# Layer four's attention: one VectorE operation a head for mask term and maximum, half the shift on GpSimd, scores one unit ahead

## What is computed

```
def attention(q, k, v, mask):                      # NH = 16 heads of HD = 16
    scores = einsum('bhqd,bhkd->bhqk', q, k) / sqrt(HD)
    scores = scores * mask - 10000.0 * (1.0 - mask)
    probs = softmax(scores, axis=-1)
    return einsum('bhqk,bhkd->bhqd', probs, v)
x = hidden + attention(self)  @ w_ao + b_ao
x = x      + attention(cross) @ w_co + b_co
return x + gelu(layernorm(x) @ w1 + b1) @ w2 + b2
```

## Time and profile before

| | us |
|---|---|
| median of 3 runs | 2088.03 (2087.43 to 2091.12) |
| the profiled execution | 2083.72 |
| its span, first to last instruction | 2082.0 |
| TensorE busy in the span | 1866.2 (90%) |
| VectorE busy | 1156.5 (56%) |
| ScalarE busy | 971.2 (47%) |
| GpSimd busy | 778.5 (37%) |

### The profile page before, as it was taken

The page is one execution under the profiler, slowest core; times in us unless marked ns, Lnnn a source line. Parts: engine busy times, 40 slices in busy tenths (PEclk is TensorE's granted clock), DMA queues, the critical chain, the costliest instruction groups (busy, mean ns, idle before and its releaser), DMA issues.

```text
span 2082.0 us, 38463 instructions
## 1 busy us (share of the span) xinstructions
PE 1866.2 (90%) x15569; PEld 1585.0 (76%) x15569; DVE 1156.5 (56%) x2107; ACT 971.2 (47%) x2550; POOL 778.5 (37%) x819
## 2 busy tenths in 40 slices
PE   6788887798999999999999999999998788888798
PEld 4566665687888888888888888888877566666587
DVE  4444544445555555556675555556544676777743
ACT  4243343334444444444444444444444466675633
POOL 3322232222342524344253343425231466675500
PEclk9899999899999999999999999999999899989899
DMA  3000001100222323132221322222120000000000
GB/s 111 11 7 2 7 2 42 47 3 11 51 57 46 67 36 77 36 61 47 41 62 36 67 46 57 56 44 54 44 82 1 11 1 2 6 1 7 1 21 21
DMA packets 163201, 71.98 MB, mean 35 GB/s; under 512 B 136512, under 2 KB 154576, under 8 KB 163024
## 3 DMA queue, kind: packets, MB, share of 16 engines
q1 hardware_dynamic: 150672, 50.64, 12.2%
q10 hardware_dynamic: 12352, 18.88, 2.9%
HBM read 33.84 MB, written 2.10 MB: 17 GB/s over the span
## 4 chain that ended last, share of the span: by engine, by line
PE 75%; DVE 10%; ACT 9%; issue 3%; POOL 2%; DMA 1%; SPq 0%; ACTq 0%; DVEq 0%; POOLq 0%
PE ps_high L197 40%; PE ps_four L197 7%; PE ps_four L2655 5%; PE ps_four L2643 5%; PE ps_four L2447 2%; PE ps_high L2539 2%; ACT l_pt L1718 1%; PE ps_high L2430 1%; PE ps_four L2455 1%; ACT l_prob L1814 1%; PE ps_high L2468 1%; ACT l_pt L1760 1%; PE ps_four L2569 1%; DVE l_sm L2156 1%; PE ps_high L2408 1%
## 5 line engine op out<-in xcount | busy, mean ns | idle before, releaser
L1824 ACT ACTIVATE l_ao<-ps_four,columns 128x512 fp32r<-128x512 f32 x128 | 87.9, 687 | 388.5 <-PE ps_four L2655 377.7
L1606 POOL TENSOR_TENSOR l_prob<-l_prob,l_mx 128x516 f32<-128x516 f32 x128 | 134.0, 1047 | 311.2 <-DVE l_mx L2198 311.2
L1814 ACT ACTIVATE l_prob<-ps_four,l_mx 128x129 f32<-128x129 f32 x512 | 181.4, 367 | 122.6 <-DVE l_mx L2191 122.5
L197 PE MATMUL ps_high<-l_hT,l_wq 128*128 128x512 f32 x768 | 211.0, 410 | 2.1 <-DVE l_hT L2079 2.1
L197 PEld LDWEIGHTS ps_high<-l_wo,l_ao 128*128 128x128 f32 x1536 | 197.6, 190 | 10.6 <-issue 0.7
L197 PE MATMUL ps_high<-l_wo,l_ao 128*128 128x256 f32 x1536 | 202.4, 281 | 0.0
L197 PE MATMUL ps_high<-l_wv,ctxT 128*128 128x512 f32 x768 | 200.7, 396 | 1.4 <-ACT l_qT L1795 1.4
L197 PE MATMUL ps_high<-ctxT,l_wk 128*128 128x512 f32 x768 | 198.3, 393 | 0.0
L1572 POOL TENSOR_TENSOR l_sm<-l_sm,l_mask 128x1024 f32<-128x1024 f32 x64 | 150.3, 2370 | 120.7 <-DVE l_sm L2156 120.6
L2204 DVE COPY l_planes<-l_prob 128x1024 uint16<-128x1024 uint16 x128 | 88.8, 694 | 148.7 <-POOL l_prob L1606 148.7
L197 PEld LDWEIGHTS ps_high<-ctxT,l_wk 128*128 128x128 f32 x768 | 144.6, 188 | 33.7 <-DVE l_V L2179 0.4
(11 more groups left out here) (295 smaller groups left out, 3857.2 us busy)
## 6 DMA issues: line engine op xcount, KB each, us to landing
l_staging<-in_L_xattn_wv ACTq DMA_DIRECT2D x8, 512.0 KB, 4.1
l_staging<-in_L_xattn_wk ACTq DMA_DIRECT2D x8, 512.0 KB, 4.3
l_staging<-in_L_xattn_wq ACTq DMA_DIRECT2D x8, 512.0 KB, 4.0
l_staging<-in_L_xattn_wo ACTq DMA_DIRECT2D x8, 512.0 KB, 3.9
ctx_tok<-in_ctx SPq DMA_DIRECT2D x8, 256.0 KB, 3.2
x_tok<-in_x SPq DMA_DIRECT2D x4, 512.0 KB, 5.1
l_raw_w<-in_L_xattn_mlp_w SPq DMA_DIRECT2D x2, 1024.0 KB, 7.5
l_planesT<-l_planes SPq DMA_TRANSPOSE x128, 3.1
```

The lines of the kernel that those rows point to most:

```text
L197: ins = e.matmul(out, a, b, start=start and i == 0, stop=stop and i == 2, skip_group_check=not check)
L1606: e.tensor_tensor(pr[:, :, 0:S + 1], pr[:, :, 0:S + 1], mx[:, 3, :].unsqueeze(2).to_broadcast([P, GB, S + 1]), ALU.mult).then_inc(sem("poo ...
L1814: ins = e.activation(pr.t[:, b, 0:S + 1], banks[b // 2].t[:, (b % 2) * (S + 2):(b % 2) * (S + 2) + S + 1], ACT.Exp, bias=mx[:, 1, b:b + 1] ...
L1824: e.activation(ao.t[:, 0, :], bk.t, ACT.Identity, bias=self.cols(f"L2_xattn_bv{at + 1}")[:, hd:hd + 1]).then_inc(sem("act.l2_values"), 1)
```

## The change

- VectorE's product with the mask stays as it is. Then, in the new stage `l3_masked`, VectorE does for each head one `tensor_tensor_reduce` of 128 x 128: it adds the mask's additive term in place and gives out the row's maximum. Eight follow the first product, eight the second, and one small operation on 128 x 8 negates the maxima that ScalarE needs. The GpSimd additions and the two VectorE maxima are gone.
- GpSimd does the shift of heads 0 to 7 (a subtraction, stage `l3_shift`) in place of VectorE.
- scores(n+1) is emitted right after probs(n-1), behind masked(n), and the transposes leave `ps_four` for single banks of the ring 4 to 7, where each is given back by its own exponential. `ps_four` now holds scores alone.
- The value copies (`l3_vv`) and the additions to x (`x_add`) are emitted a step or two later than the matmuls that they read, and the banks are given back there. `L3_RATE` goes from 2.1 to 2.3. `l3_mx` grows from 16 to 24 columns, and a spacer tile with it.

Layers one to three, the MLPs and all DMAs are the same.

```diff
-L2_SLACK, L2_SPACE = 2, (238, 18)
-L3_RATE, L3_SLACK = 2.1, 2
+L2_SLACK, L2_SPACE = 2, (238, 34)
+L3_RATE, L3_SLACK = 2.3, 2
...
         def scores(n):
             kind, g, b = self.units[n]
-            pl.slot(sm, "sm", n)
+            while (kind, g) not in begun:
+                next(rest)
             pl.bank(four, "four", "l3", n, 0)
             pl.emit("l3_scores", n, **begun[kind, g])
-            pl.free("four", "l3", n, 0)
...
+        def masked(n):
+            pl.slot(sm, "sm", n)
+            pl.slot(mx, "rowmax", n)
+            pl.emit("l3_masked", n)
+            pl.free("four", "l3", n, 0)
...
-        def probs(n):
-            pl.slot(pt, "pt", n)
-            pl.bank(four, "four", "l3", n, 1)
-            pl.emit("l3_probs", n)
-            pl.free("four", "l3", n, 1)
...
+        def probs(n, half):
+            if half == 0:
+                pl.slot(pt, "pt", n)
+            for r in (2 * half, 2 * half + 1):
+                pl.bank(over, "probT", n, r)
+                pl.emit("l3_probs", n, r)
+                pl.free("probT", n, r)
...
+        scores(0)
         for n in range(N + 2):
             if n < N:
-                while self.units[n][:2] not in begun:
-                    next(rest)
-                scores(n)
+                masked(n)
             fill()
...
             if 1 <= n <= N:
-                probs(n - 1)
+                probs(n - 1, 0)
             fill()
+            if 1 <= n <= N:
+                probs(n - 1, 1)
+            if n + 1 < N:
+                scores(n + 1)
             if n < N:
                 shifted(n)
             fill()
...
-        def l3_scores(n):
...
+        def l3_shift(n):
+
+            sm, mx = use["sm", n].t, use["rowmax", n].t
+            q.wait_ge(*pl.done("dve.l3_masked:a", n))
+            e.tensor_tensor(sm[:, 0:8, :], sm[:, 0:8, :], mx[:, 0:8].unsqueeze(2).to_broadcast([P, 8, S]), ALU.subtract).then_inc(
+                sem("pool.l3_shift"), 1)
...
+        def l3_masked(n):
...
             for i in range(2):
                 heads = bk.t[:, 2 * i:2 * i + 2, :].rearrange("p r (x t) -> p (r x) t", t=S)
-                e.tensor_tensor(sm.t[:, 8 * i:8 * i + 8, :], heads, mask.unsqueeze(1).to_broadcast([P, 8, S]), ALU.mult).then_inc(
-                    sem("dve.l3_scores:a") if i == 0 else bk.slot.empty, 1)
...
-            e.tensor_reduce(mx.t[:, 0:8], sm[:, 0:8, :], AX.X, ALU.max, negate=True).then_inc(sem("dve.l3_shift:a"), 1)
-            q.wait_ge(*pl.done("dve.l3_shift:a", n))
-            e.tensor_tensor(sm[:, 0:8, :], sm[:, 0:8, :], mx.t[:, 0:8].unsqueeze(2).to_broadcast([P, 8, S]), ALU.add).then_inc(
-                sem("dve.l3_shift:s"), 1)
-            q.wait_ge(*pl.done("pool.l3_scores", n))
-            e.tensor_reduce(mx.t[:, 8:16], sm[:, 8:16, :], AX.X, ALU.max, negate=True).then_inc(sem("dve.l3_shift:b"), 1)
...
+                e.tensor_tensor(sm.t[:, 8 * i:8 * i + 8, :], heads, mask[0].unsqueeze(1).to_broadcast([P, 8, S]), ALU.mult).then_inc(
+                    sem("dve.l3_masked:m") if i == 0 else bk.slot.empty, 1)
+                q.wait_ge(*(pl.event(("empty", "four", "l3", n, 0)) if i else pl.done("dve.l3_masked:m", n)))
+                for h in range(8 * i, 8 * i + 8):
+                    ins = e.tensor_tensor_reduce(sm.t[:, h, :], sm.t[:, h, :], mask[1], 1.0, -3.0e38, ALU.add, ALU.max, mx.t[:, h:h + 1])
+                ins.then_inc(sem("dve.l3_masked:x" if i else "dve.l3_masked:a"), 1)
+            q.wait_ge(*pl.done("dve.l3_masked:x", n))
+            e.tensor_scalar(mx.t[:, 16:24], mx.t[:, 8:16], -1.0, None, ALU.mult).then_inc(sem("dve.l3_masked:b"), 1)
```

More of the change, by code:

```diff
@@ L1281, in plan_l3 @@
         attention.close()
-        probs_done, over_done = ("full", "four", "l3", N - 1, 1), ("full", "over", "l3", N - 1)
-        self.mlp_tiles("l3e", scope, (probs_done, probs_done, over_done, ("pool.l3_scores", N - 1)))
+        probs_done, over_done = ("full", "probT", N - 1, 3), ("full", "over", "l3", N - 1)
+        self.mlp_tiles("l3e", scope, (probs_done, probs_done, over_done, ("dve.l3_masked:b", N - 1)))
         weights = self.mlp_weights("l3e", ("sp.l3_mlp", 32))
@@ new lines, in l3_masked, with l3_vv @@
+                for h in range(8 * i, 8 * i + 8):
[3 more added lines that the diff above has]
+            e.tensor_scalar(mx.t[:, 16:24], mx.t[:, 8:16], -1.0, None, ALU.mult).then_inc(sem("dve.l3_masked:b"), 1)
+        def l3_vv(t, h):
+            two_parities(use["rows", ("l3v", *t), h], use["vv", t], h, ("full", "rows", ("l3v", *t), h))
@@ L2571, in l3_scores, with l3_probs @@
             ins.then_inc(bk.slot.full, 1)
-        def l3_probs(n):
+        def l3_probs(n, r):
             sm = use["sm", n].t
-            bk = fill("four", "l3", n, 1)
-            for r in range(4):
-                q.wait_ge(*pl.done("dve.l3_shift:s" if r < 2 else "act.l3_shift", n))
-                for x in range(4):
-                    ins = e.transpose(bk.t[:, r, x * S:(x + 1) * S], sm[:, 4 * r + x, :], self.ident[:])
-                ins.then_inc(sem("pe.l3_probs") if r < 3 else bk.slot.full, 1)
+            q.wait_ge(*pl.done("pool.l3_shift" if r < 2 else "act.l3_shift", n))
+            bk = fill("probT", n, r)
+            for x in range(4):
+                ins = e.transpose(bk.t[:, x * S:(x + 1) * S], sm[:, 4 * r + x, :], self.ident[:])
+            ins.then_inc(bk.slot.full, 1)
         def l3_over(n, j):
```

84 lines of the change are left out of this document (33 added, 51 removed).

## The result

The changed kernel takes 2091.69 us (median of 20 runs, 2087.08 to 2095.96), the kernel before, run beside it on the same chip, 2087.46 us (20 runs, 2081.10 to 2093.79). The ratio is 1.0018, 95% interval 1.0010 to 1.0026: slower by some 4 us, inside the 0.2% that the prediction called "within". I had forecast 2103 us, +15 us.

A forecast was written before the change was run, and what follows sets the result against it. No engine is full; a loop of waits bounds layer four's attention, with VectorE setting the unit's length afterwards. VectorE's work +54.8 and waits -40 give +15: 2098.7 us profiled, 2103 us median, range 2044 to 2143.

The forecast's parts named there:

- removed: shift, maxima, idle for GpSimd: VectorE in layer four's attention: shift 58.7, maxima 37.7 and 37.4, idle for GpSimd 27.5 us go, 161.3 us in 31 units.
- VectorE's waits for itself: VectorE, each unit: three starts waiting 0.12 us for the result before, 0.08 us for the negation; +13.6 us in 31 units.
- standstill beside GpSimd: VectorE's heads held up by GpSimd's shift (37 us), division (11.8) and bias additions (9.9); +58.7 us together.
- That makes 0.29 us a head: VectorE's new operation per head: 0.20 us main part plus 0.09 us read of the maximum; +143.8 us for 31 x 16.
- if the read hides wholly: Lower end for VectorE's operation per head: 0.20 us a head, 99 us in all.
- rival of cheap heads: VectorE's read of the maximum runs under the next main part: 0.20 us a head, 44.6 us less, 2058 us; chance 0.23.
- I keep 15: VectorE's 55.1 us idle for scores, output projection and values falls to 15, nine of it behind value copies; -40 us.
- rival of the new wait: Banks 4 to 7, given back behind VectorE's block, idle VectorE 55 instead of 15 us: +55, 2143 us; chance 0.11.
- Half rate: Rival: VectorE's heads make a second pass over two SBUF operands, 0.42 us each: +80, 2168 us; chance 0.08.
- What would show it: Signs in the profile after: heads 0.29 us apart, ninth 1.2 us longer, VectorE busy over 90%, GpSimd 70 us lower.

The follow-up runs named there:

- e3: The changed kernel with the value copies moved from VectorE to ScalarE, at the same place of the order; 2076.92 us, ratio 0.9954 against the kernel before.
- e1: The changed kernel with GpSimd's shift of heads 0 to 7 cut from 1024 columns to 8; 2062.89 us, ratio 0.9891 against the kernel before.
- e2: The changed kernel with the shift of heads 0 to 7 moved from GpSimd to VectorE, behind its eighth head; 2095.07 us, ratio 1.0039.
- e8: The changed kernel with scores(n+1) emitted behind the first half of the transposes, ahead of `rest` and the second half; 2094.50 us, ratio 1.0028.
- e10: The changed kernel with `rest` spread by its projections, 0 to 3 a unit instead of 0 to 5; 2103.41 us, ratio 1.0077.
- e6: The changed kernel with `ps_four` in two halves and the product written back in place in PSUM, heads reading it there; 2062.03 us, ratio 0.9868.
- e4: The changed kernel with scores(n) emitted at the start of iteration n again, as in the kernel before; 2126.69 us, ratio 1.0191.

## Why the prediction was wrong, step by step

Every term had the right sign. Two of them failed in size by 38 and 34 us, in opposite senses, each because something happened otherwise than I had told it: the read of a maximum hides under the next operation, and the idle that I took off is time in which TensorE works. With the measured values the same sum reads:

| term | predicted | measured |
|---|---|---|
| removed: shift, maxima, idle for GpSimd | -161.3 | -161.3 |
| heads, 31 x 16 | +143.8 (0.29 us) | +105.6 (0.213 us) |
| VectorE's waits for itself | +13.6 | +13.6 |
| standstill beside GpSimd | +58.7 | +49.7 |
| idle for TensorE (55.1 before) | -40 (15 kept) | -6.3 (48.8 kept) |
| sum | +15 | +1.3 |

The stretch shows +0.5 us. That the forecast missed by 14 us in the sum and not by 30 to 40 is luck: the two errors have nothing to do with each other, and the rivals of either (2058 and 2143 us) each took in one of them alone.

- **"That makes 0.29 us a head"** failed. The slope of 1.04 ns a column, which gave 0.20 us for the main part, was right (0.213). The 0.09 us for the read was not: it was taken from ScalarE's pair and from small VectorE operations, and here the read's 0.08 us begins with the next head and adds at most 0.01 us (0.213 less 0.20). The lower end of my bounds, "if the read hides wholly", was the right value, and choosing the middle "since both small rows lead there" was the error: the earlier trace rows is another engine, and the earlier trace rows holds no read. The rival of cheap heads (0.23) described this term almost exactly, with 0.20 us a head.
- **"I keep 15"** failed as well. I counted mainly one kind of wait, the bank behind the value copies, and it happened, with 3.52 us of VectorE's idle at 1687 us for the 1.5 that I gave it. But e3, which takes the copies away, leaves 44.5 us, so the bulk is elsewhere. What the traces show is that VectorE idles while TensorE works on what stands ahead of the awaited result (48.1 of the 48.8 us; 4.97 us at 1763 us is a case), and that it did so before (50.9 of 55.1). It was wrong to subtract that idle because scores now *may* start early: before each scores there are still the transposes and `rest` in TensorE's queue. Nor is the late shift the cause: TensorE waited 12.0 us for it before transposes, in three units, but without it on GpSimd idle is 53.0 (e1) and 44.1 us (e2). The rival of the new wait, "as long as before, 55", was within 6 us. Neither fewer steps ahead of the scores (e8) nor fewer projections in a unit (e10) lowered it. What single cause would, if there is one, stays open.
- **The standstill** was right in kind; its size came near by luck. I had the shift begin when the eighth head is done, so that the second product covers most of it. It did so in 3 of 31 units, and there the ninth head lasted 0.95 us, 0.67 too long: with GpSimd's subtraction at 1.90 us and not the addition's 2.37, my own formula gives 0.73 (1.90 + 0.08 - 1.25), 23 us in 31 units. In the other units the shift came late, mostly behind a division that waited for ScalarE. 20 shifts met a head, the late ones mostly past the product's cover, and cost 1.4 us each on average; 11 began so late that VectorE was idle or at a layer norm, a copy, an addition, a product or the negation. Together that is 28.7 us for 37. The divisions gave 4.3 for 11.8, the biases 15.9 for 9.9. e1 shows that it lay on the path (its stretch is 25.2 us shorter), e6 that it comes from two SBUF inputs (none left with one in PSUM). The rule of the Trainium skill, "SBUF — State Buffer", section "Who interferes with whom", agrees with both: the heads with two SBUF inputs waited for GpSimd's instruction to end (1962.15 against 1962.00 us), those with one did not (none over 0.30 us in e6). The same section has tensor_scalar, copy and cast among the operations that can enter a two-port mode and contend for the port even with one input; the negation, a tensor_scalar that waited 1.88 us in e6, agrees with it.
- **Half rate** did not occur: with both sources in SBUF and float32 a head starts 0.213 us after the last, with one in PSUM just the same. The rule of the Trainium skill that I weighed there ("Vector Engine (DVE) Microarchitecture Reference", "Points that are easy to get wrong") did not show for this operation.
- **The waits of VectorE for itself** were right: product to first head 1.26 us (1660.77 to 1662.03, 1663.73 to 1664.99), for 1.13 + 0.12. With heads 0.077 us dearer each the last unit (7.64 us to its negation) would have come to 8.87 us, near the 8.9 that I gave a unit, but in part by luck: its standstill was 1.6 us instead of 1.2, and it met no division, for which the 8.9 hold some 0.4.
- **What would show it**: heads closer than 0.25 us and VectorE idle for more than 30 us were both named as signs against the prediction, and both came. VectorE was busy for 84% of the stretch, not over 90. GpSimd's busy time fell by 106 us, not 70: besides additions less shifts (some 86 us), its division went from a mean of 1336 to 758 ns. VectorE's long shift, beside which it lasted 1.72 us in the earlier trace rows, is no longer there.
- **Outside the stretch** nothing was forecast. The two profiles' spans differ by 8.2 us, the medians by 4.2, the stretch by 0.5; where the remaining 4 us of the medians come from, single executions can't tell, and it stays open.

## What to carry to other kernels

- An operation with a second instruction that only reads out a result costs what its main part costs, if that read starts with the next main part; look in the trace for two instructions with the same start before adding durations. When no row shows it, the lower bound deserves its own weight, not a point between neighbours of another kind.
- Idle time that comes from another engine's order of work did not go away here because one edge of it was moved. Before crediting it, list what is still queued ahead of the awaited instruction; where such a list is long, start from the idle that was there and credit only what you can name.
- When one engine's work is to be covered by another's, ask when the other engine's queue reaches it, not only when its input is ready. Here GpSimd's shift stood behind a division that waited for ScalarE, and began 0.6 to 11.6 us late in 28 of 31 units.
- If VectorE and GpSimd work side by side, ask of each VectorE operation how many inputs it has in SBUF. Moving one into PSUM (here the product written back in place) removed 54 us of standstill from the heads, of which more idle and longer negations took back 21, for 21 us more of TensorE time, at least 15 of which were hidden. It gave the fastest kernels of the study that leave nothing out: 2062 and 2059 us, ratio 0.987.

## What the runs showed of the hardware that I had not expected

- The read of a maximum out of VectorE (0.08 us) starts together with the next head or product in 465 of 496 cases, and these follow 0.213 us behind the head. The other 31 stand before the negation, which needs the maxima and starts 0.32 us behind the last head.
- Like the one on four columns in the earlier trace rows, a one-input operation on 8 columns in SBUF was held up by GpSimd: it lasted 1.88 us beside the shift, 0.17 alone, while two-input heads with one input in PSUM ran freely beside such a shift.
- GpSimd's subtraction with a broadcast column takes 1.90 us for 1024 columns, its addition of a full tile 2.37, the biases 2.36 to 2.43 (means of the three kinds).
- Moving a delay changes when two engines meet: with the same instructions, the standstill was 49.7 us in one order (the change) and 69.9 in another (e10), while the idle was 48.8 and 47.0. In e4 it was the idle that moved more (72.8 us), with the standstill at 64.0.
- After a wait of 4.86 us TensorE ran at a granted clock of 0.50 (1.2 GHz), and the scores that VectorE was waiting for took 2.09 us instead of 1.17: in this place the wait cost something behind it as well.
